# A two-layer graph network on one core: edge rows four iterations behind the node rows instead of three

## The reference

```
h = max(layernorm(x), 0)
x = x + attention(h)      # per edge: leaky logits of h[src] and h[dst], softmax over the edges
                          # of one dst, h[src] @ W_embed weighted and summed into dst;
                          # per node: + h @ W_lin + bias
h = max(layernorm(x), 0)
x = x + h + messages(h)   # per edge: MLP of [h[src], h[dst], bond] times sigmoid(bond @ Wa),
                          # summed into src
```

## Time and profile before

| | |
|---|---|
| median of 3 runs | 1449.07 us (1445.94 to 1449.92) |
| profiled execution | 1441.65 us |
| its span | 1439.9 us |
| busy in the span | DVE 1165.9, POOL 1087.7, PE 1050.7, ACT 772.7 us |
| indirect gathers of the row stage | 392, in four groups by buffer |
| last `take` of the row stage | starts at 520.58 us, ends at 520.86 us |

### The profile page before, as it was taken

How to read it: one execution, slowest core, us unless ns; L and a number is a source line. 1 busy time by engine, 2 the same in 40 slices (tenths; PEclk the granted TensorE clock), 3 DMA queues, 4 the chain that set the end, 5 groups by cost and what they waited for, 6 DMA issues and landing times.

```text
span 1439.9 us, 23870 instructions
## 1 busy us (share of the span) xinstructions
PE 1050.7 (73%) x6191; PEld 805.2 (56%) x6191; DVE 1165.9 (81%) x3896; ACT 772.7 (54%) x2040; POOL 1087.7 (76%) x984
## 2 busy tenths in 40 slices
PE   5777777778777756555564696767888888878874
PEld 3665555556565646555554364445656666656553
DVE  7999999999999999888889685556776777777652
ACT  3999988988988966655555232222222222222221
POOL 6777777777777717777777777878788888888885
PEclk9999999999999976877766598999998998999887
DMA  5788877877787655555554333333333333333332
GB/s 153 227 269 246 252 243 235 266 232 248 246 251 232 213 161 183 179 173 175 179 178 140 92 52 57 52 47 53 52 54 51 55 55 54 53 53 54 49 40 29
DMA packets 182160, 202.71 MB, mean 141 GB/s; under 512 B 25033, under 2 KB 134609, under 8 KB 182025
## 3 DMA queue, kind: packets, MB, share of 16 engines
q1 hardware_dynamic: 124111, 129.55, 27.7%
q0 software_dynamic: 56240, 71.10, 25.3%
q10 hardware_dynamic: 1674, 0.53, 0.2%
HBM read 90.62 MB, written 109.66 MB: 139 GB/s over the span
## 4 chain that ended last, share of the span: by engine, by line
POOL 51%; issue 18%; PE 11%; DVE 10%; DMA 6%; ACT 2%; ACTq 1%; SPq 0%; POOLq 0%; DVEq 0%
POOL out_dram L1297 14%; POOL out_dram L1199 12%; POOL XE L1283 7%; POOL XN L183 5%; POOL XE L183 5%; POOL O L183 4%; POOL R L183 4%; PE bank L1594 4%; DMA XE<-out_dram,gidx 3%; DVE st L541 2%; DVE BD L579 1%; PE bank L1543 1%; PE bank L1547 1%; DVE st L546 1%; DMA out_dram<-BS,sx 1%
## 5 line engine op out<-in xcount | busy, mean ns | idle before, releaser
L1199 POOL DMA_INDIRECT out_dram<-BD,BS x196 | 202.4, 1033 | 90.6 <-issue 58.5
L1283 POOL DMA_INDIRECT XE<-out_dram,gidx x188 | 187.6, 998 | 60.1 <-issue 52.8
L794 ACT ACTIVATE BD<-BD,nmr,rstd 128x128 f32<-128x128 f32 x392 | 171.7, 489 | 41.3 <-DVE nmr L562 41.3
L1146 PE MATMUL bank<-BD 128*128 128x128 f32 x392 | 110.3, 377 | 114.3 <-DVE BD L1017 114.3
L1297 POOL DMA_INDIRECT out_dram<-BS,sx x100 | 159.0, 1590 | 38.9 <-issue 30.9
L1297 POOL DMA_INDIRECT out_dram<-TS,sx x96 | 152.7, 1590 | 32.6 <-issue 28.7
L868 PE MATMUL bank<-wes,TS 128*128 128x132 f32 x392 | 99.2, 336 | 104.7 <-ACT TS L805 104.2
L1363 DVE TENSOR_SCALAR H<-bank,key 128x512 f32<-128x512 f32 x132 | 98.8, 748 | 87.8 <-PE bank L1510 87.8
L1146 PEld LDWEIGHTS bank<-BD 128*128 128x128 f32 x392 | 86.8, 273 | 125.2 <-issue 125.2
L868 PEld LDWEIGHTS bank<-wes,TS 128*128 128x128 f32 x392 | 60.1, 193 | 150.8 <-ACT TS L805 147.0
L1594 PEld LDWEIGHTS bank<-XN,H 128*128 128x128 f32 x1056 | 125.1, 195 | 18.0 <-issue 16.5
(11 more groups left out here) (238 smaller groups left out, 2997.0 us busy)
## 6 DMA issues: line engine op xcount, KB each, us to landing
out_dram<-BD SPq DMA_DIRECT2D x96, 512.0 KB, 3.4
BD<-out_dram SPq DMA_DIRECT2D x1024, 0.5 KB
base_rows<-BD SPq DMA_DIRECT2D x49, 256.0 KB, 4.6
BD<-base_rows SPq DMA_DIRECT2D x49, 256.0 KB, 3.4
H<-BD SPq DMA_DIRECT2D x49, 256.0 KB, 3.2
XN<-in_x_dram SPq DMA_DIRECT2D x13, 512.0 KB
BD<-bond_rows SPq DMA_DIRECT2D x49, 128.0 KB, 2.2
bond_rows<-in_edge_attr_dram SPq DMA_DIRECT2D x50, 125.0 KB
```

Source lines behind the costliest of these rows:

```text
L794: last = nc.scalar.activation(OT[u][:, g, w:w + D], OT[u][:, g, w + D:w + 2 * D], ACT.Relu, bias=nmr[:, slot, t:t + 1], scale=rstd[:, slot ...
L1146: nc.tensor.matmul(ps[6][:, 0:D], DG[u][:, c, :], BS4[u][:, c, :], start=first, stop=final, skip_group_check=True)
L1199: pool.indirect_dma_start(out, bass.IndirectOffsetOnAxis(sidx[:, it * G4 + c:it * G4 + c + 1], 0), RO4[u][:, c, :], None, bounds_check=lim ...
L1283: pool.indirect_dma_start(XS4[u][:, c, :], None, halves, bass.IndirectOffsetOnAxis(gidx[:, j, 0:1], 0), bounds_check=None, oob_is_err=Fals ...
```

## The change

AHEAD goes from 3 to 4. There are now four iterations with nodes alone (0 to 3), 45 with both (4 to 48), and four with edges alone (49 to 52). Every gather, spill and edge instruction goes with its edge set to the next iteration; the number of gathers and of buffers stays. The first set now lies in the buffer XN instead of XE. The two other edits extend a table for the added iteration and let ACT's wait for node scales end where the node rows end.

```diff
-        AHEAD = 3
+        AHEAD = 4
         STOP = ITS + AHEAD
...
         def late_turn(it):
-            return ITS + (3, 5, 6)[it - ITS]
+            return ITS + (3, 5, 6, 7)[it - ITS]
...
-                    if g == 0 and it + 1 < STOP:
+                    if g == 0 and (ahead(it + 1) or nodes(it - 2)):
                         act.wait_ge(norm_ready, it + 2 if ahead(it + 1) else rows_turn(it + 1))
```

## The result

| | before | after |
|---|---|---|
| median | 1446.4 us (1445.08 to 1449.92, 7 runs) | 1454.46 us (1451.77 to 1457.12, 7 runs) |
| ratio | | 1.0053, 95% interval 1.0036 to 1.0070 |
| profiled execution, its span | 1441.65, 1439.9 us | 1451.77, 1450.1 us |
| last gather starts | 507.97 | 514.57 |
| last `take` ends | 520.86 | 530.15 |

The change makes the kernel slower, by 0.53% or about 8 us (the interval is 5 to 10 us). The traces differ by 9.3 us at the end of the row stage, by 9.3 at the first scatter and by 10.2 over the span, so what follows passes the shift on, as forecast, within 0.9 us. The profiled execution of the kernel before, 1441.65 us, lies 3.4 us under the fastest of its seven runs, so the two traces stand further apart than the two medians.

The account below looks back on a forecast made before the run. The row stage was taken to be bound by POOL's unbroken gather stream. A 5.5 us stall, less 0.2 slack and 1.0 in the drain, gave +4.3 us on 1449.07, so 1453.4 us, range 1448.8 to 1457.5.

Parts of the forecast that it names:

- The stall: POOL's wait ahead of its 33rd gather, for take(4,0) in place of take(3,0): 5.5 us, bounds 4.6 to 7.6.
- the 3.0 us that DVE saves: Work DVE drops before take(3,0); ACT and PE running close behind would let 2.1 us of it through.
- The node-only iteration: Iteration 3 after the change: smaller takes without a logits copy bring 9.45 us down to 8.6.
- Slack at the last gather: Time between the last gather's landing and DVE measuring its rows: 0.2 us, taken off the stall.
- The drain: From measuring the last rows to the last take: 1.0 us shorter, bounds 0 and 1.5, with less node work left.
- the split costs nothing: Extra small operations of the split iterations, some 2 us, cost nothing because edge-only iterations 49 and 50 wait for POOL.
- Rival 1: Stall at full size: ACT dates take(4,0), so the 3.0 us saved ahead are lost; about +7 us, chance 0.12.
- Rival 2: Stall hidden: the drain was DVE's, its slack swallows the stall; -0.3 to +2 us, chance 0.10.
- Rival 3: POOL's pace changes as gathers meet fewer or more two-input DVE operations; down to -6.0 us, chance 0.10.
- My count of the chances: Argument that gathers meet two-input DVE operations by chance: 85 of 392 gathers, against 190 operations filling a quarter of 500 us.

Follow-up runs that it names:

- e11: Kernel before (AHEAD 3) gathering only source rows from the fifth set on; 1501.45 against 1630.37 us, ratio 0.9228 (0.919 to 0.9265), slower chip.
- e4: Changed kernel plus ten unread PE transposes ahead of the first group of each edge-only iteration; ratio 0.9997 (0.9974 to 1.0019) against the kernel before, slower chip.
- e5: The changed kernel as it is, on a slower chip: 1631.94 against 1630.07 us for the kernel before, ratio 1.0008 (0.9987 to 1.0030).
- e6: The kernel before, unedited, run for its trace on one of the slower chips, where it takes 1627 to 1630 us.
- e9: Kernel before (AHEAD 3) with add_rows adding only 8 of 128 columns on DVE; ratio 0.9996 (0.9967 to 1.0025) against the kernel before, slower chip.
- e12: Changed kernel (AHEAD 4) gathering only source rows from the fifth set on; 1508.80 us, ratio 0.9261 (0.9202 to 0.9321) against the kernel before, slower chip.

## Why the prediction came out as it did

**The number.** Forecast 1453.4 us, measured 1454.46, in the range and on the slower side. That they agree so well is in part luck. The forecast was 1449.07 + 4.3, and seven runs put the kernel before at 1446.4; the change cost 8.1 us, nearly twice the 4.3. That is outside the band of +2.5 to +6.5 to which I gave 0.68, though the interval, 5 to 10 us, reaches into it.

**Held.** That on the first chip the row stage is bound by POOL's unbroken stream; that the change puts one stall at the 33rd gather and no other of size; that the last gather is later by the stall; that no slack in the drain hides it; that all behind the stage shifts by the same amount. This rests on the two traces of that chip, since no experiment ran on it. e11 fits: with half of the gathers, on another chip, DVE took 9.69 us an iteration from 16 to 46, ((485.54 - 194.75) / 30), below the first chip's 10.24.

**The stall: 5.5 forecast, 6.65 measured**, within its bounds. take(3,0) came at 44.41 and not 43.6, so 1.3 of the 3.0 us that DVE saves got through ACT and PE and not 2.1. The node-only iteration took 8.85 us, not 8.6. And between the end of take(4,0), 53.81, and POOL's start at 54.08 lie 0.27 us that I had left out.

**Slack at the last gather: 0.2 forecast**, 0.5 measured. From its start to the measurement of its rows were 3.1 us before and 2.56 after, where DVE waits 0.79 us for it.

**The drain: -1.0 forecast, +3.2 measured.** This is the step that failed, outside its own bounds of 0 and 1.5. I wrote that the last iteration's takes are paced by PE in both, and took PE's pace for the same. It was 1.83 us a group after the change and 1.0 before, as the granted clock was 0.50 and 1.00. The sum is 6.6 - 0.5 + 3.2 = +9.3 and not +4.3. With it failed the sentence that iterations 49 and 50 wait for POOL, so that the split costs nothing: the trace has no gather wait in them but the 0.79 us at 517.13, and PE was busy all the time from 510 to 525 us. Eight groups lie behind 517.13; at e4's pace with the clock at 1.00 (5.0 us from take(51,0) to take(52,0), then 3.6 to the last) they would end near 517.54 + 5.0 + 3.6 + 0.3 = 526.4, an estimate, 3.7 us sooner. The term would then be -0.5, inside its bounds. So the clock is the likely cause of 3.7 of the 5.0 us by which the end of the row stage missed the forecast, argued from one trace each and not tested on that chip. By this estimate the kernel would lose 5.6 us with the clock up, and the interval of the medians, 5 to 10 us, holds both 5.6 and 9.3. Why the clock stayed low after one wait and came back after the other is not settled. On the other chips it comes and goes without pattern, too: at 645 to 650 us it is 0.57 in e5 and 0.50 in e6, then 1.00 and 0.50.

**Rival 1**, the full stall, was about as near for the stall (7.6 against 5.5, measured 6.65): of the 3.0 us that it has lost, 1.3 were saved. The medians' +8.1 is nearer to its +7 than to my +4.3, but its sum held no lost clock. **Rival 2**, a hidden stall, is dead on the first chip: 6.6 us reach the last gather. On the other chips it is what happens, though by another mechanism, as POOL waits for DVE anyway. **Rival 3**, another pace of POOL: 39 long gathers against 41, 383.2 us busy against 382.9; nothing. Its mechanism got support in e9, where the long gathers inside the additions vanish. My count of the chances was wrong: there are 49 + 98 = 147 of these operations and not 190, 100 us or a fifth of the time, which is just the share of the gathers that start in one (85 of 392). Of those 85, 36 are long. The 49 others all start 0.55 us or more into the operation of 0.68 us. The Trainium skill (SBUF — State Buffer, Who interferes with whom) says that a DVE instruction with two SBUF inputs contends with a GpSimd instruction that reads SBUF, and the trace agrees; the price is about 0.2 us a meeting early in the operation.

## What to carry to other kernels

If an engine streams without a gap from the first to the last item of a stage, a one-time wait near its start is paid in full at the end (6.65 us of wait, 6.6 at the last gather); so look, for each buffer that such a stream reuses, at the date on which it is freed. Running one stage further ahead splits an iteration into a fill part and a drain part, and the sum of the two is longer than the whole (8.7 + 5.0 or more against 9.6 us in e12): it must buy something. And take an engine's pace in a drain from rows at either level of its clock, for the drain is where gaps let it fall.

## What the runs showed of the hardware

- The same program took 1446 us in the first measurements and 1627 to 1630 on the five chips of the experiments. On those, gathers issued by POOL hold up the rest: in an unbroken stream PE and DVE all but stand and no other queue moves (28 to 47 us); with eight gathers an iteration takes 12.5 us, with four 9.6, with none (while POOL stands) 9.45. The idle time is put down to "issue" and "remote". Whether the engines lack instructions, or loads, or both, is open; no run here tells it apart.
- In the kernel before, all 33 gathers that start in the first half microsecond of a two-input DVE operation of 0.68 us take over 1.0 us, 1.17 at the median, in place of 0.95. Of the 52 that start later in one, 49 take their usual time.
- PE's clock fell to 1.2 GHz beside a wait of 1.65 us in both traces of the first chip. In one it came back after 3 us; in the other it stayed down for the last 25 us of the stage, with PE busy without a break from 506 to 529 us. On the slower chips it averaged 0.82 from 300 to 400 us with all gathers (e6) and 1.00 with half of them (e11).
